# Head softmax on one core: GpSimd issues its adding DMA ahead of the weighing of an older unit

## The chip, the core and the metric

The kernel runs on one core of one Trainium2 chip. The metric is the device time of one execution in microseconds (us). Four compute engines matter here: TensorE (PE; its weight loads are PEld), VectorE (DVE), ScalarE (ACT) and GpSimd (POOL). SyncE (SP) only issues DMAs. Each engine runs its own list of instructions in order; engines wait for each other on semaphores.

## The reference, cut to what matters

Two transformer layers on x of 4 x 1024 x 128: banded attention, a mixture of 32 experts, a second attention, and the experts again. Only the second attention is touched. Its softmax runs over the **heads**, not over the keys:

```
q = (x @ Wq.T + bq).reshape(B, S, H, D)              # 16 heads of 8
scores = jnp.einsum('bqnd,bknd->bnqk', q, k) / jnp.sqrt(jnp.float32(D))
attn = jax.nn.softmax(scores, axis=1)                # axis 1: the heads
out = jnp.einsum('bnqk,bknd->bnqd', attn, v)
```

So for every pair of a query and a key, 16 exponentials are summed over the heads, and each is divided by that sum.

## The kernel before

The stage is `head_softmax_attention`. Its work is cut into **units**: 128 keys by 128 queries by 16 heads. A chunk is one tile of 128 queries; it has 8 units, one for each tile of keys (`kt` 0 to 7). There are 4 batches of 8 chunks, so 32 chunks and `ALL` = 256 units. Each engine walks over the units with its own lag:

- **TensorE**, `chunk_of`: in its unit u it subtracts the maximum from the first half of the scores (`take_maximum`, line 912), makes the scores of the second half (`scores_of`, line 890), sums the quarters of unit u-4 into the denominator (`denominator_of`, line 922), makes the first half of the scores of u+1, subtracts the second maximum, and multiplies the weights of unit u-5 with the values (`attend`, line 905). At some `kt` the function `ahead` adds projections of later chunks and, at `kt` 6, the output of the chunk before (lines 928, 929).
- **ScalarE**: the exponential of the first half of unit u (line 1069), the copy of heads 0 to 7 of unit u-1 from `ex` to `half` (`copy_heads`, line 1032), for unit u-4 the logarithm of the denominator and two exponentials that make reciprocals, one in PSUM for VectorE (`recp`, line 1041) and one in SBUF for GpSimd (`recip`, line 1043), then the exponential of the second half of unit u.
- **VectorE**: the maxima of both halves (`largest`, line 1115), then heads 0 to 9 of unit u-4 times the reciprocal (`weigh`, line 1122), then now and then a small operation of `ahead`.
- **GpSimd**: three things for each step, each of another unit. `add_halves` (line 847) issues a DMA that adds heads 8 to 15 of `ex` onto the copy in `half`, inside SBUF; it waits for `copy_heads`. `add_quarters` (line 853) waits for that DMA to land and adds the upper half of `half` onto the lower, which leaves four slabs for TensorE. `weigh_rest` (line 859) waits for `recip` and weighs heads 10 to 15.

So one unit passes through copy, DMA, quarters, denominator, reciprocal, weighing and product with the values. `ex` has 6 buffers, `half` has 4, `recip` has 2. The order on GpSimd is written out by hand. In step s, before the change:

```
weigh_rest(s - 4)      # behind recip of unit s-4
add_halves(s - 1)      # behind the copy of unit s-1; issues its DMA
add_quarters(s - 2)    # behind the landing of the DMA of unit s-2
```

Of the kernel before, what the change touches and what calls it, by code (L numbers as in the profile page):

```python
# [715 lines left out]
def head_softmax_attention(nc, c, x, mv, ht, q_dram, k_dram, k_first, zero_f16, zero_f32):  # L716
# [8 lines left out]
    LAG, RING, SUMS = 4, 6, 4  # L725
    ON_DVE = 10
    BY_DMA = 0
    ALL = B * NQ * BT
# [4 lines left out]
    with Mem(nc, "head") as m:  # L733
# [39 lines left out]
        def copies(unit):  # L773

            return 3 * unit + (4 if unit < ALL - 1 else 3)
# [64 lines left out]
        @block.gpsimd  # L840
        def _(pool):
            m.start(pool, "pool")

            def add_halves(unit):

                pool.wait_ge(ex_ready, ONE + copies(unit))
                pool.dma_start(half[:, unit % SUMS, :, :], ex[:, unit % RING, 8:16, :], accum_op=ALU.add).then_inc(summed[unit % 2], 16)  # L847

            def add_quarters(unit):

                pool.wait_ge(summed[unit % 2], (unit // 2 + 1) * 16)
                hf = half[:, unit % SUMS, :, :]
                pool.tensor_tensor(hf[:, 0:4, :], hf[:, 0:4, :], hf[:, 4:8, :], ALU.add).then_inc(quarter_ready, 1)  # L853

            def weigh_rest(unit):

                pool.wait_ge(copy_ready, ONE + unit + 1)
                e = ex[:, unit % RING, ON_DVE:NH, :]
                pool.tensor_tensor(e, e, recip[:, unit % 2, :][:, None, :].broadcast_to([P, NH - ON_DVE, P]),  # L859
                                   ALU.mult).then_inc(rest_ready, 1)  # L860

            for step in range(ALL + LAG):
                if step >= LAG:
                    weigh_rest(step - LAG)
                if 0 < step <= ALL:
                    add_halves(step - 1)
                if 1 < step <= ALL + 1:
                    add_quarters(step - 2)

        @block.tensor  # L870
        def _(pe):
# [813 lines left out]
def build(nc, drams, x_dram, out):  # L1685
    with ExitStack() as ctx:
        c = {n: ctx.enter_context(nc.sbuf_tensor(f"c_{n}", s, dt)) for n, (s, dt) in SHAPES.items()}
        x = ctx.enter_context(nc.sbuf_tensor("x_tokens", [P, NT, E], F32))
        for n in WEIGHTS:
            c[n] = ctx.enter_context(nc.sbuf_tensor(f"c_{n}", [P, WEIGHTS[n], 2, P], F16))  # L1690
        for att in ("a_", "b_"):
            c[att + "bias"] = ctx.enter_context(nc.sbuf_tensor(f"c_{att}bias", [P, 2], F32))
        c["a_out"] = ctx.enter_context(nc.sbuf_tensor("c_a_out", [P, E], F32))

        mv = ctx.enter_context(nc.sbuf_tensor("moments", [P, NT, 2], F32))
        w_dram = nc.dram_tensor("pair_weights", [NPAIR, 2, T], F32).ap()

        q_dram = nc.dram_tensor("a_queries", [P, SLOTS, QCOLS], F16).ap()
        k_dram = nc.dram_tensor("a_keys", [P, SLOTS, KCOLS], F16).ap()
        v_dram = nc.dram_tensor("a_values", [LEFT + T + VTAIL, E], F32).ap()  # L1700
        with Mem(nc, "att_a") as m:
            bt = BandTensors(m)
            banded_attention(nc, c, x, mv, bt, q_dram, k_dram, v_dram, x_dram, drams)
        feed_forward(nc, "ffn1", c, x, mv, w_dram, True)
        bq_dram = nc.dram_tensor("b_queries", [P, SLOTS, P], F16).ap()
        bk_dram = nc.dram_tensor("b_keys", [P, SLOTS, P], F16).ap()
        zero_f16, zero_f32 = drams["zero_f16"], drams["zero_f32"][0:BT * (NH + 1) * VSLOT]
        bk_first = nc.dram_tensor("b_keys_first", [S // BLK, P, SLOTS, BLK], F16).ap()
        with Mem(nc, "att_b") as m:
            ht = HeadTensors(m)  # L1710
            head_softmax_attention(nc, c, x, mv, ht, bq_dram, bk_dram, bk_first, zero_f16, zero_f32)
        feed_forward(nc, "ffn2", c, x, mv, w_dram, False, out)
# [72 lines left out]
```

## Time and profile before

| | us |
|---|---|
| median of 3 runs | 1948.12 |
| their range | 1943.28 to 1952.0 |
| the profiled execution's own time | 1951.87 |
| its span, first to last instruction | 1950.1 |
| granted TensorE clock, mean over the span | 0.968 of full speed |

The profile page gives busy time by engine over the whole span; the stage in question lies between about 545 and 1641 us of it. Times in rows are us from the start of the span unless marked ns. In a timeline a row is start, duration, engine, line, operation, what it writes and reads, and in brackets how long the engine had been idle and who ended that. A GpSimd record can overlap the one before it by up to 0.3 us, so starts are the better measure there.

### The profile page before, as it was taken

The numbers are of one execution on the slowest core, as the hardware profiler recorded it, in microseconds if no ns is written. First come the engines' busy times: TensorE is split into PE (matmuls) and PEld (weight loads), VectorE is DVE, ScalarE is ACT, GpSimd is POOL, SyncE is SP. The second block draws the span as 40 slices with busy tenths as digits, with TensorE's granted clock in tenths as the row PEclk, the third lists the DMA queues.
The fourth block names the chain that finished last, engine by engine and source line by source line (L and its number), as shares of the span: only waits on it lengthen the run. The fifth ranks groups of instructions, "written<-read, shape, count | busy, mean of one in ns | idle before, by whom it ended". The sixth has DMA issues, their size and how long they took to land. (4 is left out here: it accounts for less than half of the span.)

```text
span 1950.1 us, 52397 instructions
## 1 busy us (share of the span) xinstructions
PE 1835.9 (94%) x20664; PEld 1154.3 (59%) x20664; DVE 1653.7 (85%) x2601; ACT 1434.7 (74%) x2473; POOL 1443.5 (74%) x1180
## 2 busy tenths in 40 slices
PE   5999799999789999999999999999999997999998
PEld 3666644444346666666666666666666665544443
DVE  6777688887679999999999999999999995788776
ACT  4566456666568888888888888888888884566665
POOL 6245256565349999999999989989999997456565
PEclk8999699999879999999999999999999997899999
DMA  6644176765267777777777667777767772677673
GB/s 162 195 110 105 27 150 140 135 141 113 81 140 141 143 136 140 136 139 139 139 136 142 133 134 144 139 136 139 137 125 138 135 134 56 130 151 154 124 133 56
DMA packets 156741, 253.07 MB, mean 130 GB/s; under 512 B 54736, under 2 KB 86368, under 8 KB 155760
## 3 DMA queue, kind: packets, MB, share of 16 engines
q0 software_dynamic: 36864, 134.23, 36.7%
q1 hardware_dynamic: 114112, 112.89, 26.7%
q8 instruction: 164, 2.69, 0.6%
q10 hardware_dynamic: 5520, 2.60, 0.5%
q14 instruction: 81, 0.66, 0.1%
HBM read 96.95 MB, written 18.55 MB: 59 GB/s over the span
## 5 line engine op out<-in xcount | busy, mean ns | idle before, releaser
L1115 DVE TENSOR_REDUCE head_shift<-head_score 128x64 bf16<-128x1024 f32 x512 | 625.8, 1222 | 74.4 <-PE head_score L890 48.2
L1069 ACT ACTIVATE head_ex<-head_score 128x1024 f32<-128x1024 f32 x512 | 521.1, 1018 | 121.5 <-PE head_score L912 120.9
L859 POOL TENSOR_TENSOR head_ex<-head_ex,head_recip 128x768 f32<-128x768 f32 x256 | 491.0, 1918 | 7.3 <-ACT head_recip L1043 6.6
L1371 POOL TENSOR_TENSOR ffn_sw<-ffn_sg,ffn_wide 128x512 f32<-128x512 f32 x256 | 324.9, 1269 | 218.4 <-ACT ffn_sg L1482 203.7
L853 POOL TENSOR_TENSOR head_half<-head_half 128x512 f32<-128x512 f32 x256 | 359.4, 1404 | 70.1 <-DMA head_half<-head_ex 67.8
L1122 DVE TENSOR_TENSOR head_ex<-head_ex,head_recp 128x1280 f32<-128x1280 f32 x256 | 378.2, 1477 | 10.0 <-ACT head_recp L1041 10.0
L912 PE MATMUL head_score<-head_shift,c_identb 128*128 128x512 bf16 x1024 | 311.7, 386 | 17.0 <-DVE head_shift L1115 11.7
L890 PE MATMUL head_score<-att_b_HB,att_b_GR 96*128 96x256 f16 x2048 | 312.4, 275 | 1.4 <-ACT head_ex L1069 1.4
L922 PE MATMUL head_den<-head_half,c_ident 128*128 128x128 f32 x2048 | 281.6, 281 | 20.2 <-POOL head_half L853 19.3
L847 POOL DMA_DIRECT2D head_half<-head_ex x256 | 251.2, 981 | 47.3 <-ACT head_half L1032 47.3
L905 PE MATMUL head_outp<-head_ex,att_b_vs 128*32 128x128 f32 x8192 | 277.4, 277 | 0.0
L922 PEld LDWEIGHTS head_den<-head_half,c_ident 128*128 128x128 f32 x2048 | 251.6, 193 | 39.4 <-POOL head_half L853 36.1
L905 PEld LDWEIGHTS head_outp<-head_ex,att_b_vs 128*32 128x32 f32 x8192 | 210.2, 110 | 107.0 <-issue 106.7
L1032 ACT ACTIVATE head_half<-head_ex 128x1024 f32<-128x1024 f32 x256 | 268.6, 1049 | 0.0
L1616 DVE TENSOR_TENSOR ffn_hidden<-ffn_sw,ffn_up 128x512 f32<-128x512 f32 x256 | 178.2, 696 | 93.1 <-POOL ffn_sw L1371 86.6
L1482 ACT ACTIVATE ffn_sg<-ffn_gate 128x512 f32<-128x512 f32 x272 | 162.4, 597 | 115.8 <-PE ffn_gate L116 114.7
L890 PEld LDWEIGHTS head_score<-att_b_HB,att_b_GR 96*128 96x128 f16 x2048 | 189.0, 98 | 88.2 <-ACT head_ex L1069 40.1
L1487 ACT ACTIVATE ffn_h_parts<-ffn_hidden 128x512 f16<-128x512 f32 x272 | 162.5, 597 | 97.4 <-DVE ffn_hidden L1616 90.6
L1624 DVE TENSOR_TENSOR ffn_h_parts<-ffn_hidden,ffn_h_parts 128x512 f16<-128x512 f32 x272 | 186.0, 684 | 0.1
L912 PEld LDWEIGHTS head_score<-head_shift,c_identb 128*128 128x128 bf16 x1024 | 66.9, 98 | 107.7 <-DVE head_shift L1115 83.9
L114 PE MATMUL ffn_down<-ffn_h_parts,c_down_parts 128*128 128x512 f16 x272 | 103.2, 379 | 3.3 <-DVE ffn_h_parts L1624 3.3
L114 PE MATMUL ffn_up<-ffn_xnT,c_up_parts 128*128 128x512 f16 x272 | 104.0, 382 | 0.6 <-DVE ffn_hidden L1616 0.3
(265 smaller groups left out, 2538.7 us busy)
## 6 DMA issues: line engine op xcount, KB each, us to landing
head_half<-head_ex POOLq DMA_DIRECT2D x256, 512.0 KB, 5.0
ffn_wide<-pair_weights SPq DMA_DIRECT2D x256, 256.0 KB, 9.7
band_v_windows<-a_values SPq DMA_DIRECT2D x24, 192.0 KB, 4.8
att_b_vs<-in_zero_f SPq DMA_DIRECT2D x2, 2176.0 KB, 10.0
a_keys<-band_parts_k SPq DMA_DIRECT2D x12, 295.5 KB, 2.5
att_a_HB<-a_keys SPq DMA_DIRECT2D x48, 73.9 KB
a_queries<-band_parts_q SPq DMA_DIRECT2D x12, 271.5 KB, 2.9
att_a_GR<-a_queries SPq DMA_DIRECT2D x12, 271.5 KB
```

What stands on the lines that cost most here:

```text
L847: pool.dma_start(half[:, unit % SUMS, :, :], ex[:, unit % RING, 8:16, :], accum_op=ALU.add).then_inc(summed[unit % 2], 16)
L853: pool.tensor_tensor(hf[:, 0:4, :], hf[:, 0:4, :], hf[:, 4:8, :], ALU.add).then_inc(quarter_ready, 1)
L859: pool.tensor_tensor(e, e, recip[:, unit % 2, :][:, None, :].broadcast_to([P, NH - ON_DVE, P]), ALU.mult).then_inc(rest_ready, 1)
L890: last = pe.matmul(score[:, h, g // 2, (g % 2) * GH * QS:(g % 2 + 1) * GH * QS].rearrange("p (a w) -> p a w", a=GH), GR[:, buf, g, kt * P: ...
L905: last = pe.matmul(outp[g * 32:(g + 1) * 32, 0:P], vs[:, buf * BT + kt, at:at + 32], ex[:, unit % RING, i, :], start=(kt == 0 and n4 == 0) ...
L912: last = pe.matmul(score[:, h, k, :].rearrange("p (a w) -> p a w", a=NH // 2), c["identb"][:, :], shift[:, h, :][:, None, :].broadcast_to( ...
L922: last = pe.matmul(den[:, 0:P], c["ident"][:, :], half[:, unit % SUMS, k, :], start=(i == 0), stop=(i == len(SLABS) - 1))
L1032: act.activation(half[:, unit % SUMS, BY_DMA:8, :], ex[:, unit % RING, BY_DMA:8, :], ACT.Copy).then_inc(ex_ready, 1)
L1069: act.activation(ex[:, unit % RING, :, h * QS:(h + 1) * QS].rearrange("p (a g) w -> p g a w", g=NG), score[:, h, :, :].rearrange("p k (g a ...
L1115: dve.tensor_reduce(shift[:, h, :], score[:, h, :, :].rearrange("p k (a w) -> p w k a", a=NH // 2), AX.XY, ALU.max, negate=True).then_inc( ...
L1122: dve.tensor_tensor(e, e, recp[:, 0:P][:, None, :].broadcast_to([P, ON_DVE, P]), ALU.mult).then_inc(prob_ready, 1)
L1371: pool.tensor_tensor(sw[:, unit % 2, :], sg[:, unit % 2, :], wide[:, k % 2, i, :], ALU.mult).then_inc(sw_ready, 1)
```

## The change

On GpSimd the weighing moves from the front of the step to its middle. Nothing else is changed: no size, no buffer, no instruction more or fewer, no other engine. The last steps are written out, so that the quarters of the last unit come ahead of the last three weighings.

```diff
@@ -859,13 +859,16 @@
                 pool.tensor_tensor(e, e, recip[:, unit % 2, :][:, None, :].broadcast_to([P, NH - ON_DVE, P]),
                                    ALU.mult).then_inc(rest_ready, 1)
 
-            for step in range(ALL + LAG):
+            for step in range(ALL + 1):
+                if step > 0:
+                    add_halves(step - 1)
                 if step >= LAG:
                     weigh_rest(step - LAG)
-                if 0 < step <= ALL:
-                    add_halves(step - 1)
-                if 1 < step <= ALL + 1:
+                if step > 1:
                     add_quarters(step - 2)
+            add_quarters(ALL - 1)
+            for unit in range(ALL + 1 - LAG, ALL):
+                weigh_rest(unit)
```

## Rows read from the trace of the kernel before

**Rows 1.** The page: busy time by engine, and two groups of the stage.
```profile
span 1950.1 us, 52397 instructions
PE 1835.9 (94%) x20664; PEld 1154.3 (59%) x20664; DVE 1653.7 (85%) x2601; ACT 1434.7 (74%) x2473; POOL 1443.5 (74%) x1180
...
L859 POOL TENSOR_TENSOR head_ex<-head_ex,head_recip 128x768 f32<-128x768 f32 x256 | 491.0, 1918 | 7.3 <-ACT head_recip L1043 6.6
...
L853 POOL TENSOR_TENSOR head_half<-head_half 128x512 f32<-128x512 f32 x256 | 359.4, 1404 | 70.1 <-DMA head_half<-head_ex 67.8
```

**Rows 2.** Windows: us, busy us of each engine, granted clock, DMA share, GB/s.
```profile
600.00:700.00 100.00, 98.17 (x1293) 68.23 (x1291) 95.34 (x92) 88.77 (x155) 94.15 (x74) 1.00 0.73 140
...
1100.00:1200.00 100.00, 96.24 (x1272) 66.77 (x1264) 92.49 (x90) 86.62 (x150) 92.57 (x72) 1.00 0.72 139
```

**Rows 3.** The tile head_half: landing of the DMA, and who waited (us, times).
```profile
L853 POOL TENSOR_TENSOR head_half<-head_half x256: 1257/1377/1592, 559.8 to 1630.0; 128x512 f32<-128x512 f32 x128
...
  PEld head_den L922: 36.1, 66
  PE head_den L922: 19.3, 29
  ACT head_lnd L1038: 16.4, 18
...
DMA to landing us min/median/max: 4.5/5.0/6.9
```

**Rows 4.** Timeline, all engines, a late landing and what followed.
```profile
867.00 0.97 POOL L847 DMA_DIRECT2D head_half<-head_ex  x1
...
869.08 1.97 POOL L859 TENSOR_TENSOR head_ex<-head_ex,head_recip 128x768 f32<-128x768 f32 x1
...
870.84 1.05 POOL L847 DMA_DIRECT2D head_half<-head_ex  x1
...
873.54 1.26 POOL L853 TENSOR_TENSOR head_half<-head_half 128x512 f32<-128x512 f32 x1 [1.65 <-DMA head_half<-head_ex]
...
874.77 1.81 POOL L859 TENSOR_TENSOR head_ex<-head_ex,head_recip 128x768 f32<-128x768 f32 x1
...
874.86 1.16 PE L922 MATMUL head_den<-head_half,c_ident 128*128 128x128 f32 x8 [0.56 <-POOL head_half L853]
...
876.49 1.23 DVE L1115 TENSOR_REDUCE head_shift<-head_score 128x64 bf16<-128x1024 f32 x1 [0.89 <-PE head_score L890]
```

**Rows 5.** Timeline, VectorE: the weighing of four units (24, 232 and 240 units after the first).
```profile
601.84 1.48 DVE L1122 TENSOR_TENSOR head_ex<-head_ex,head_recp 128x1280 f32<-128x1280 f32 x1
...
700.97 1.48 DVE L1122 TENSOR_TENSOR head_ex<-head_ex,head_recp 128x1280 f32<-128x1280 f32 x1
...
1574.71 1.48 DVE L1122 TENSOR_TENSOR head_ex<-head_ex,head_recp 128x1280 f32<-128x1280 f32 x1
...
1606.92 1.48 DVE L1122 TENSOR_TENSOR head_ex<-head_ex,head_recp 128x1280 f32<-128x1280 f32 x1
```

**Rows 6.** Timeline, all engines, a stretch without a late denominator.
```profile
931.94 1.48 DVE L1122 TENSOR_TENSOR head_ex<-head_ex,head_recp 128x1280 f32<-128x1280 f32 x1
...
933.86 1.05 ACT L1032 ACTIVATE head_half<-head_ex 128x1024 f32<-128x1024 f32 x1
...
934.81 0.87 POOL L847 DMA_DIRECT2D head_half<-head_ex  x1
...
935.33 0.29 ACT L1043 ACTIVATE head_recip<-head_lnd 128x128 f32<-128x128 f32 x1
...
935.42 1.57 POOL L853 TENSOR_TENSOR head_half<-head_half 128x512 f32<-128x512 f32 x1
...
936.66 2.10 POOL L859 TENSOR_TENSOR head_ex<-head_ex,head_recip 128x768 f32<-128x768 f32 x1
...
937.46 1.06 PE L922 MATMUL head_den<-head_half,c_ident 128*128 128x128 f32 x8
...
938.15 1.05 ACT L1032 ACTIVATE head_half<-head_ex 128x1024 f32<-128x1024 f32 x1
...
938.42 1.18 POOL L847 DMA_DIRECT2D head_half<-head_ex  x1
...
939.51 1.08 PE L905 MATMUL head_outp<-head_ex,att_b_vs 128*32 128x128 f32 x32
```

**Rows 7.** Line 859, all 256: duration in ns, min, median, max.
```profile
L859 POOL TENSOR_TENSOR head_ex<-head_ex,head_recip x256: 1800/1828/2126, 568.9 to 1634.4; 128x768 f32<-128x768 f32 x128
```

**Rows 8.** Timeline, all engines, the end of the stage.
```profile
1615.57 2.08 POOL L859 TENSOR_TENSOR head_ex<-head_ex,head_recip 128x768 f32<-128x768 f32 x1
...
1617.31 1.05 ACT L1032 ACTIVATE head_half<-head_ex 128x1024 f32<-128x1024 f32 x1
...
1620.01 1.06 ACT L1032 ACTIVATE head_half<-head_ex 128x1024 f32<-128x1024 f32 x1
...
1625.19 1.13 POOL L847 DMA_DIRECT2D head_half<-head_ex  x1
...
1627.41 1.97 POOL L859 TENSOR_TENSOR head_ex<-head_ex,head_recip 128x768 f32<-128x768 f32 x1
...
1630.05 1.26 POOL L853 TENSOR_TENSOR head_half<-head_half 128x512 f32<-128x512 f32 x1 [0.67 <-DMA head_half<-head_ex]
...
1631.37 2.07 PE L922 MATMUL head_den<-head_half,c_ident 128*128 128x128 f32 x8 [1.62 <-POOL head_half L853]
...
1633.37 6.08 PE L905 MATMUL head_outp<-head_ex,att_b_vs 128*32 128x128 f32 x160
...
1634.43 1.83 POOL L859 TENSOR_TENSOR head_ex<-head_ex,head_recip 128x768 f32<-128x768 f32 x1 [1.35 <-ACT head_recip L1043]
```

## The prediction

> **What bounds the stage now.** I read the page first. Over the span PE is busiest, but GpSimd's quarters (line 853) carry 67.8 us of waiting for their own DMA, while its weighing waits 6.6 us [rows 1]. The windows of the stage show PE and VectorE both above 92% at full clock, GpSimd about as full, and no engine quite at 100 [rows 2]. Such a picture is a ring of engines that pass one unit round, so I asked which wait starts the others. The rows of the tile `head_half` show it: the DMA takes 4.5 to 6.9 us to land, 5.0 in the median, and PE's denominator waited for the quarters in 66 and 29 records, 55 us together [rows 3].
>
> The timeline shows one such case from end to end [rows 4]. The DMA issued at 867.00 belongs to the quarters at 873.54: 6.54 us apart, because landing was late, and GpSimd stood idle for 1.65 us with the next weighing queued behind. PE's denominator started at 874.86, right behind the quarters; PE's scores followed it, and VectorE then sat idle for 0.89 us. Without such a case VectorE goes round in 4.1 us and is nearly full.
>
> There is a closed loop in the old order. Within a step GpSimd issues DMA u only after a weighing, and the weighing only after quarters u-2, which wait for DMA u-2. So two units can't take less than landing 5.0, plus quarters to weighing 1.23 (873.54 to 874.77), plus weighing to issue 1.76 (869.08 to 870.84) [rows 3, 4]: 8.0 us, or 4.0 a unit. A landing of 5.5 already makes 4.25. This is as long as the period of the other engines, so each late landing tells.
>
> **What the stage would take without these waits.** VectorE's weighing marks the units. Three chunks in a row, 24 units from 601.84 to 700.97, show no loss at all: 99.13 us, 33.04 a chunk, 4.13 a unit. In the last batch, which projects no keys or values ahead, an undisturbed chunk took 32.21 (1574.71 to 1606.92) [rows 5]. From 601.84 to 1606.92 there are 30 chunks in 1005.08 us. Of these 23 lie before the last batch and 7 in it: 23 x 33.04 + 7 x 32.21 = 985.4. The excess is 19.7 us, and I put it down to late quarters.
>
> **The change, part by part.** No instruction is added or removed. In the new order DMA u comes directly behind quarters u-2, and the weighing behind the DMA.
>
> *The DMA is issued earlier.* Its copy has long been ready: the issue at 938.42 is for the copy that ended at 934.91, 3.5 us before [rows 6]. The new loop for two units is 5.0 + 1.23 = 6.2 us, or 3.1 a unit, far below 4.0 (and a 6.9 us landing makes 4.1). Between issue u and quarters u now lie a weighing, quarters, an issue and another weighing, over a full period. In the clean stretch, with issues some 0.1 us behind their copies, 4.1 us apart, the quarters come about 2.7 us behind the next issue, so 6.8 us behind their own: only the longest landing is late, by 0.1.
>
> *Does GpSimd have room?* Near the end it runs nearly free: three units from 1615.57 to 1627.41 take 11.84 us, 3.95 each [rows 8]. That is less than 4.13, and 0.08 less than the last batch's 4.03. GpSimd will therefore catch up with ScalarE and wait for the copy instead, at the head of a step. This idle time costs nothing as long as the round holds.
>
> *What is queued behind that new wait.* The weighing, then the quarters. Take the copy that ended at 934.91 [rows 6]. Issue 935.0; its record is 0.87 long, so the weighing runs from about 935.9 (its reciprocal is ready at 935.62, 0.71 behind the copy) to 937.7, quarters to 938.9. The product that takes this weighing starts at 939.51, so 1.8 us of room where the old order had 0.75 (936.66 + 2.10 = 938.76). The denominator that takes these quarters is one period behind the one at 937.46, at about 941.6: 2.7 us of room. The issue is next wanted at the following copy's end, 939.20, and GpSimd is free at 938.9. Nothing is late; the smallest reserve is this last 0.3 us.
>
> *Does the moved weighing get dearer beside other work?* The page says 1918 ns in the mean, and the 256 records run from 1800 to 2126 ns [rows 1, 7], but two of different length (1.97 and 2.10) both have the next start 1.76 behind [rows 4, 6]; the rest is overlap in the records. Phases against VectorE vary through the stage in the old run, so the new phase costs nothing: 0 us, with a bound of 0.3 us x 256 = 77 us if all were paid at the long record's length. I take 0.
>
> By the Trainium skill, "SBUF — State Buffer", the section on the shared port pair, a VectorE operation with two SBUF inputs locks out GpSimd; VectorE's weighing takes its reciprocal from PSUM, and the narrow spread of starts agrees that nothing is blocked.
>
> *The tail.* The last copy ends at 1621.07, its DMA is issued only at 1625.19, quarters at 1630.05, denominator 1631.37, products 1633.37 to 1639.45 [rows 8]. In the new order the last issue waits for quarters that follow one weighing: the copy before it ended at 1618.36, so issue 1618.5, weighing to 1621.1, quarters to 1622.35, last issue 1622.35. It lands 5.0 later, at 1627.35; quarters to 1628.6; the denominator starts 2.8 us earlier than before. Three weighings now stand behind the last quarters, 1628.6 + 3 x 1.77 = 1633.9; the denominator ends 2.0 behind its start, at 1630.6, and the products of five units take 6.08, so the last unit's begin at about 1635.5. Hidden; 2.8 us gained.
>
> **Sum.** 19.7 + 2.8 = 22.5 us. On the profiled execution's own 1951.87 that gives 1929.4. That execution lies 3.75 above the median of the runs shown; from the median the same sum gives 1925.6. Part of the spread of those runs should be luck in landings, which the change takes away, so I take a value between, 1928. The rest of the program isn't touched.
>
> **Rivals.**
>
> *The wait only moves, no change.* The 19.7 us might not be GpSimd's: VectorE and PE, over 92% busy, could hold the round by themselves and the idle time could be theirs. For it: PE has its own pauses behind the scores. Against: the three clean chunks ran with the same PE and VectorE work [rows 5]. If half of the excess stays, the time is 1948 - 10 = 1938; if nearly all, 1943 to 1948.
>
> *The transfer is hidden anyway.* Then quarters never wait, and the reorder is worth 0, 1948 us. The row says 67.8 us of waits and 5.0 us for the landing [rows 1, 3], against it. By the Trainium skill, "DMA: Bandwidth & Descriptors", the section on the anatomy of one DMA, a transfer takes about 2.0 us plus its bytes over 436 GB/s; for these 512 KB that would be 3.2 us, an estimate by the page, and no quarters would wait. This trace disagrees, with 4.5 as the least.
>
> *GpSimd becomes the bound, slower.* The issue now waits for ScalarE at the head of a step, and each such wait empties GpSimd's queue, so the overlaps of 0.3 us in the records are lost, as would be any time between a semaphore and a start. At 3.95 + 0.1 it still fits. From 4.13 on it decides; the old mean, 1005.08 / 240 = 4.19 [rows 5], is break-even. At 3.95 + 0.3 + 0.1 = 4.35 the stage takes 0.16 x 256 = 41 us more, 1989. Against: after a DMA wait the old run restarts with start-to-start 1.23 and 1.76, no more [rows 4]. Its point is near, so it isn't nothing.
>
> *More than the sum.* If other engines' hidden waits for late quarters went as well, the 4.13 could fall to the last batch's 4.03: another 0.1 x 184 = 18 us, 1910. Against: that batch has less work ahead.
>
> **How the numbers follow.** The forecast has 0.72, between 1920 and 1936. Half or none of the gain (the first two rivals together) has 0.17, GpSimd as the bound 0.07, more than the sum 0.04. The range 1918 to 1943 takes in the forecast and about half of the first rival, 0.82. A measurement of this kernel can tell about 0.5%, so 9.7 us, from no change. Faster by more: 0.72 + 0.04 + a little of the half case, 0.77; within: 0.16; slower: 0.07.
>
> **What the new profile would show.** Right: line 853 waits for its DMA almost never; line 847 now waits for the copy (line 1032), 0.1 to 0.3 us in most units; PE's and PEld's waits for `head_half` fall from 55 us to a few in the tail; chunks of 33.0 us throughout, 32.2 in the last batch; the stage shorter by some 22 us with landings still near 5.0. Wrong: the chunks stay at 33.5 with new pauses of PE behind line 859 or of VectorE behind line 1041, or GpSimd without idle time at over 4.13 a unit, or landings that grow because two DMAs overlap longer.

## The result, and the profile after

The changed kernel takes 1931.76 us in the median of 5 runs (1926.64 to 1932.25), against 1948.12 us of 5 runs before (1943.07 to 1952.0). The ratio is 0.9915, 95% interval 0.989 to 0.994: 0.6 to 1.1% faster. The forecast was 1928, range 1918 to 1943. The profiled execution took 1932.25 us against 1951.87.

Lines from 862 on have moved by 3: 1069 is now 1072, 1122 is 1125, 922 is 925, 905 is 908. First the page of the changed kernel:

```profile
span 1930.4 us, 52397 instructions
PE 1826.9 (95%) x20664; PEld 1150.4 (60%) x20664; DVE 1655.3 (86%) x2601; ACT 1425.5 (74%) x2473; POOL 1452.1 (75%) x1180
...
L859 POOL TENSOR_TENSOR head_ex<-head_ex,head_recip 128x768 f32<-128x768 f32 x256 | 551.4, 2154 | 0.2 <-ACT head_recip L1046 0.2
...
L853 POOL TENSOR_TENSOR head_half<-head_half 128x512 f32<-128x512 f32 x256 | 405.7, 1585 | 0.7 <-DMA head_half<-head_ex 0.7
...
L847 POOL DMA_DIRECT2D head_half<-head_ex x256 | 234.5, 916 | 93.2 <-ACT head_half L1035 85.6
```

The same group in the page of the kernel before:

```profile
L847 POOL DMA_DIRECT2D head_half<-head_ex x256 | 251.2, 981 | 47.3 <-ACT head_half L1032 47.3
```

The wait of the quarters for their DMA has gone from 67.8 us to 0.7 [rows 1], and the issue now waits for its copy, which is what the new head of the step should do. Before, its 47.3 us were 3 waits at the very start of the stage; now 49.9 us are such a start, and 35.1 us are 91 short waits between 600 and 1585 us. The landing itself is no faster than before [rows 3], and who waited for `head_half` shows that the wait did not simply move to TensorE. The tile `head_half` of the changed kernel:

```profile
  PEld head_den L925: 5.7, 3
  PE head_den L925: 4.6, 2
...
DMA to landing us min/median/max: 4.5/5.1/7.1
```

TensorE waited 55 us for the quarters before, in 95 records; now 10 us in 5, all at the end of the stage. The weighings of VectorE mark the units, at the same four places as in [rows 5] (timeline of the changed kernel):

```profile
603.32 1.48 DVE L1125 TENSOR_TENSOR head_ex<-head_ex,head_recp 128x1280 f32<-128x1280 f32 x1
...
702.46 1.48 DVE L1125 TENSOR_TENSOR head_ex<-head_ex,head_recp 128x1280 f32<-128x1280 f32 x1
...
1558.10 1.48 DVE L1125 TENSOR_TENSOR head_ex<-head_ex,head_recp 128x1280 f32<-128x1280 f32 x1
...
1590.33 1.48 DVE L1125 TENSOR_TENSOR head_ex<-head_ex,head_recp 128x1280 f32<-128x1280 f32 x1
```

The first two marks are 24 units and 99.14 us apart; before they were 99.13, since this was the clean stretch. Over the 30 chunks from the first mark to the last it is 987.01 us for 1005.08: 18.1 us less. Over the first three batches the mean chunk is 33.03 us, so the clean chunk of 33.04 now holds there throughout, and nothing has become quicker than it; in the last batch it is 32.5.

How GpSimd now walks (timeline of the changed kernel, GpSimd alone):

```profile
904.16 0.88 POOL L847 DMA_DIRECT2D head_half<-head_ex  x1 [0.33 <-ACT head_half L1035]
904.83 2.06 POOL L859 TENSOR_TENSOR head_ex<-head_ex,head_recip 128x768 f32<-128x768 f32 x1
906.62 1.49 POOL L853 TENSOR_TENSOR head_half<-head_half 128x512 f32<-128x512 f32 x1
908.09 0.88 POOL L847 DMA_DIRECT2D head_half<-head_ex  x1
908.70 2.12 POOL L859 TENSOR_TENSOR head_ex<-head_ex,head_recip 128x768 f32<-128x768 f32 x1
910.49 1.56 POOL L853 TENSOR_TENSOR head_half<-head_half 128x512 f32<-128x512 f32 x1
912.66 0.88 POOL L847 DMA_DIRECT2D head_half<-head_ex  x1 [0.61 <-ACT head_half L1035]
```

The DMA issued at 904.16 belongs to the quarters at 910.49, 6.3 us later, with a weighing, other quarters, an issue and one more weighing between. A landing of 5.1 us, the median, is over 1.2 us before the quarters begin. The idle time of 0.3 or 0.6 us stands ahead of the issue, where it costs nothing. The records of the weighing have grown from 1918 to 2154 ns and those of the quarters from 1404 to 1585, yet nothing is slower: starts are still 1.79 apart from weighing to quarters. A GpSimd record begins while the one before still runs, so the busy time of the weighing's line has grown by 60 us without any more work; GpSimd as a whole shows 1452.1 us for 1443.5.

The end of the stage (timeline of the changed kernel, all engines):

```profile
1605.66 1.19 POOL L847 DMA_DIRECT2D head_half<-head_ex  x1
...
1610.58 1.26 POOL L853 TENSOR_TENSOR head_half<-head_half 128x512 f32<-128x512 f32 x1 [0.68 <-DMA head_half<-head_ex]
1611.81 3.58 POOL L859 TENSOR_TENSOR head_ex<-head_ex,head_recip 128x768 f32<-128x768 f32 x2
...
1612.55 2.05 PE L925 MATMUL head_den<-head_half,c_ident 128*128 128x128 f32 x8 [0.52 <-ACT head_lnd L1041]
...
1614.53 5.34 PE L908 MATMUL head_outp<-head_ex,att_b_vs 128*32 128x128 f32 x160
...
1619.94 0.28 ACT L1051 ACTIVATE head_outT<-head_outp 128x128 f32<-128x128 f32 x1 [4.43 <-PE head_outp L908]
```

From the last mark to the copy of the output it is 1619.94 - 1590.33 = 29.6 us. Before, with the same copy at 1639.53, it was 32.6: 3.0 us less. Counted from that mark, the last quarters start 2.9 us earlier (20.25 us behind it for 23.13 [rows 8]), but the last denominator only 2.2 us (22.22 for 24.45), because it now waits for the logarithm of the one before. The rest is in the 160 products, which take 5.34 us for 6.08. In both kernels they begin at a granted clock of 0.50 (1.2 GHz), after a stretch in which TensorE idled between denominators (in the changed kernel it was busy 1.16 of the 4.5 us from 1605.0 to 1609.5, the last before the clock fell). In the changed kernel the clock came back sooner: 0.67 in the mean from 1614.5 to 1617.0 us and 1.00 after it, against 0.50 from 1633.4 to 1636.0 and 0.92 up to 1639.4 before.

### The profile page after: what moved, and what is told of

Read it like the earlier page. It is cut to its first block and busy times, and to the rows that moved or that the text cites. A ratio compares the mean times of both kernels' runs of the same rounds, so it can differ in the third digit from the quotient of the medians.

```text
span 1930.4 us, 52397 instructions
## 1 busy us (share of the span) xinstructions
PE 1826.9 (95%) x20664; PEld 1150.4 (60%) x20664; DVE 1655.3 (86%) x2601; ACT 1425.5 (74%) x2473; POOL 1452.1 (75%) x1180
## 5 line engine op out<-in xcount | busy, mean ns | idle before, releaser
L859 POOL TENSOR_TENSOR head_ex<-head_ex,head_recip 128x768 f32<-128x768 f32 x256 | 551.4, 2154 | 0.2 <-ACT head_recip L1046 0.2
L853 POOL TENSOR_TENSOR head_half<-head_half 128x512 f32<-128x512 f32 x256 | 405.7, 1585 | 0.7 <-DMA head_half<-head_ex 0.7
L1125 DVE TENSOR_TENSOR head_ex<-head_ex,head_recp 128x1280 f32<-128x1280 f32 x256 | 378.2, 1477 | 7.7 <-ACT head_recp L1044 7.7
L847 POOL DMA_DIRECT2D head_half<-head_ex x256 | 234.5, 916 | 93.2 <-ACT head_half L1035 85.6
L925 PE MATMUL head_den<-head_half,c_ident 128*128 128x128 f32 x2048 | 272.8, 277 | 5.1 <-POOL head_half L853 4.6
```

The source lines that it names most:

```text
L925: last = pe.matmul(den[:, 0:P], c["ident"][:, :], half[:, unit % SUMS, k, :], start=(i == 0), stop=(i == len(SLABS) - 1))
L1125: dve.tensor_tensor(e, e, recp[:, 0:P][:, None, :].broadcast_to([P, ON_DVE, P]), ALU.mult).then_inc(prob_ready, 1)
```

## The experiments

Each ratio is against runs of the kernel before on the same chip; chips differ between groups of experiments, so ratios compare better than medians. "Mean chunk" is the distance of VectorE's marks 8 and 248, 30 chunks, divided by 30; it was 33.50 us before and is 32.90 with the change. "Quarters wait for DMA" is the time that line 853 waited for a landing, in us over the whole execution. "Tail" is from mark 248 to the copy of the output. These three are each read from one profiled execution.

| run | us, median | ratio (95%) | mean chunk | quarters wait for DMA | tail |
|---|---|---|---|---|---|
| the change | 1931.76 | 0.9915 (0.989 to 0.994) | 32.90 | 0.7 | 29.6 |
| e1_body_only | 1931.05 | 0.9916 (0.9893 to 0.9938) | 32.90 | 0.9 | 31.2 |
| e2_old_half_dma | 1932.91 | 0.9917 (0.9903 to 0.9932) | 32.90 | 0.3 | 30.7 |
| e3_new_half_dma | 1931.33 | 0.9909 (0.9893 to 0.9925) | 32.90 | 0 | 30.1 |
| e4_issue_quarters_weigh | 1955.0 | 1.0039 (1.0022 to 1.0056) | 33.71 | 63.2 | 29.9 |
| e5_new_ahead_early | 1913.15 | 0.9834 (0.9811 to 0.9856) | 32.34 | 0.7 | 30.0 |
| e6_old_ahead_early | 1941.53 | 0.9979 (0.9963 to 0.9995) | 33.25 | 63.2 | 31.6 |
| e7_new_on_dve_9 | 1952.73 | 1.004 (1.0022 to 1.0058) | 33.53 | 0.4 | 32.7 |
| e8_new_on_dve_11 | 1949.22 | 1.0024 (1.001 to 1.0037) | 33.53 | 1.2 | 28.9 |
| e9_early_and_tail | 1912.94 | 0.9838 (0.9814 to 0.9862) | 32.33 | 1.0 | 29.9 |
| e10_early_tail_both | 1911.04 | 0.981 (0.9783 to 0.9837) | 32.34 | 0.3 | 27.1 |

Two theories were put against each other. **The landing theory**: in the old order two units cannot take less than landing + quarters + weighing, about 8.0 us, and late landings held up the round. **The rival**: what helps is that the DMA is issued first in the step, ahead of a weighing, whatever the landing.

**e1_body_only.** The new steps with the old end.

```diff
-            add_quarters(ALL - 1)
-            for unit in range(ALL + 1 - LAG, ALL):
+            weigh_rest(ALL + 1 - LAG)
+            add_quarters(ALL - 1)
+            for unit in range(ALL + 2 - LAG, ALL):
                 weigh_rest(unit)
```

> The new order in every step but the old order of the last ones: the weighing of unit 253 stands ahead of the quarters of unit 255 again. The landing theory (late landings held the round, and the tail is a small separate term) expects chunks of 33.04 us as with the full change, and an end of the stage within 1.5 us of the full change's, since the weighing fills the 0.7 us in which GpSimd waited for the last landing: 1930 to 1934 us. The rival that the new tail carries a good part of the gain expects 1938 or more.

The chunks are the change's, to 0.01 us. The tail is 31.2 us, 1.5 more than with the change and 1.5 less than before. That isn't the worth of the new end, though. The last denominator of e1 starts 22.60 us behind the mark, only 0.4 us later than with the change; the other 1.1 us are in its products (timeline of e1, TensorE):

```profile
1609.30 2.07 PE L926 MATMUL head_den<-head_half,c_ident 128*128 128x128 f32 x8 [0.89 <-POOL head_half L853]
1611.30 6.47 PE L909 MATMUL head_outp<-head_ex,att_b_vs 128*32 128x128 f32 x160
```

They take 6.47 us for 5.34, at a granted clock of 0.50 from 1611.3 to 1614.0 and 0.84 from there to 1617.8. So of the 2.2 us by which the change's last denominator is earlier, about 1.8 come from the new steps and 0.4 from the new end; the rest of the tail is TensorE's clock. In the time of the whole none of this can be seen. It is the body that makes the gain.

**e2_old_half_dma, e3_new_half_dma.** The transfer is halved, in the old and in the new order. Heads 12 to 15 are left out of the denominator, so these two kernels don't compute the reference's result; every other instruction stays.

```diff
-                pool.dma_start(half[:, unit % SUMS, :, :], ex[:, unit % RING, 8:16, :], accum_op=ALU.add)...
+                pool.dma_start(half[:, unit % SUMS, 0:4, :], ex[:, unit % RING, 8:12, :], accum_op=ALU.add)...
```

> The old order with the adding DMA cut to heads 8 to 11, 256 KB for 512 KB; heads 12 to 15 are left out of the denominator. The landing theory: with about 3.5 to 4 us of landing for 5.0 the loop over two units shrinks from 8.0 to below 7.0 us, so the old order too runs in chunks of 33.0 us, quarters hardly wait, and the time is 1929 to 1935 us. The rival (what helped is that the issue no longer stands behind the weighing, whatever the landing) expects no change, 1944 to 1950.

> The new order with the same half-size DMA (heads 12 to 15 left out of the denominator). The landing theory: landing has left the round, so nothing more is won in the chunks, 33.04 us each, and at most 1 or 2 us in the tail: 1928 to 1932. If the transfer still cost something in the new order, or DMA traffic slowed other engines, it would be below 1925.

The old order with the half-size DMA, the tile `head_half`, and its timeline on GpSimd:

```profile
  PE head_den L922: 5.6, 3
...
DMA to landing us min/median/max: 3.3/3.4/5.1
```

```profile
905.04 1.83 POOL L859 TENSOR_TENSOR head_ex<-head_ex,head_recip 128x768 f32<-128x768 f32 x1 [0.49 <-ACT head_recip L1043]
906.81 0.86 POOL L847 DMA_DIRECT2D head_half<-head_ex  x1
907.42 1.56 POOL L853 TENSOR_TENSOR head_half<-head_half 128x512 f32<-128x512 f32 x1
908.81 1.95 POOL L859 TENSOR_TENSOR head_ex<-head_ex,head_recip 128x768 f32<-128x768 f32 x1
```

With a landing of 3.4 us the old order runs in the same chunks as the new one. Its weighing waits for the reciprocal at the head of the step (0.49 us), the mark of an engine that is ahead, and its issue still stands behind the weighing. The new order gains nothing from the short transfer. So landing time is what the old order was held by, and what the new one takes off the round. The rival falls. Of the 1 or 2 us that e3 was allowed to gain in the tail nothing came: its last denominator starts 22.22 us behind the mark, as with the change, and its tail is 30.1 us for 29.6 because the products took 5.77 us.

**e4_issue_quarters_weigh.** Issue first as in the change, but the weighing last.

```diff
-                if step >= LAG:
-                    weigh_rest(step - LAG)
                 if step > 1:
                     add_quarters(step - 2)
+                if step >= LAG:
+                    weigh_rest(step - LAG)
```

> In each step issue, quarters, weighing: the issue comes first as in the new order, but the quarters that wait for the last landing follow at once and the weighing is behind them. The landing theory: the loop over two units is again landing 5.0 + quarters 1.23 + weighing 1.77 = 8.0 us, and the weighing ends later than in the old order, at the limit of what the product with the values wants: no faster than before, 1945 to 1975. The rival that it is enough to issue first expects 1928 to 1935.

It is 0.4% slower than before. Who waited for line 859, none in the kernel before, and the waits for the DMA (of this run, two views of lines and tiles):

```profile
who waited for it (us, times):
  PEld head_outp L908: 18.1, 30
  PE head_outp L908: 10.0, 16
```

```profile
its engine sat idle before it (us, times) until:
  DMA head_half<-head_ex: 63.2, 93
  ACT head_half L1035: 56.5, 23
```

Both halves of the expectation are there. The order around the ring (weighing, issue, quarters) is the old one, with the weighing a place later; the loop over two units is unchanged, and so is the wait for the DMA. The weighing is so late that the product with the values waits for it, 28 us in 46 records. What the change has right is not that the issue is first, but that a weighing lies between an issue and the quarters of the unit before.

**e5_new_ahead_early, e6_old_ahead_early.** On TensorE, `ahead` goes where TensorE waits for a maximum.

```diff
+                    ahead(b, q, kt)
                     take_maximum(unit, 1)
...
                         attend(unit - (LAG + 1), n - 1 if back else n, (kt - LAG - 1) % BT, 1 - buf if start and back else buf)
-                    ahead(b, q, kt)
```

> The new order, and on TensorE the projections and outputs of other chunks are put ahead of the second maximum, where TensorE waits for VectorE by 0.3 to 0.4 us in most units, rather than behind the product with the values. If the clean chunk of 33.04 us is set by TensorE and VectorE in turn, with TensorE's extra work on that path, four units of a chunk lose 0.15 us or so and the one with the output up to 0.4: chunks of 32.2 to 32.6, 1914 to 1925 us. If VectorE alone sets it (it has small extra operations in six of the eight units), little changes: 1927 to 1932. If GpSimd, 3.9 a unit, is the next bound, chunks stay at or above 31.6.

> The same move on TensorE with the old order on GpSimd. The landing theory: the loop of 8.0 us for two units, 32.0 a chunk plus late landings, does not move, so less is won than in the new order, 0 to 10 us, and waits for the DMA grow over the 67.8 us of the kernel before: 1938 to 1948. If landing did not hold the old order, this would win as much as the same move in the new order.

With the new order this is worth another 0.8%, and 1913.15 us lies 0.85 below the range that was expected. The waits between 600 and 1500 us; the changed kernel first:

```profile
PEld head_score L915 <- DVE head_shift L1118: 77.6, 238, 0.6
POOL head_half L847 <- ACT head_half L1035: 34.6, 90, 0.6
```

```profile
PEld head_score L915 <- DVE head_shift L1118: 51.2, 190, 0.6
...
POOL head_half L847 <- ACT head_half L1035: 8.2, 26, 0.3
```

The second fence is e5's. The wait of TensorE's weight loads for the maximum is used up by a third, the undisturbed chunk is 32.38 us (633.08 to 665.46 on VectorE) for 33.04, and GpSimd's spare time falls from 34.6 to 8.2 us, so GpSimd is now nearly a bound. With the old order (e6) the same move shortens the mean chunk by only 0.25 us, not 0.56, and wins 0.2%. TensorE's and the weight loads' waits for the quarters in e6 come to 22.9 and 47.6 us over the whole, 70 for 55: the gain runs into the landing. One detail of the expectation was wrong: GpSimd's own wait for the DMA did not grow, it was 63.2 us. The late quarters show at TensorE instead.

**e7_new_on_dve_9, e8_new_on_dve_11.** One head moved from VectorE to GpSimd, and the other way.

```diff
-    ON_DVE = 10
+    ON_DVE = 9
```

In e8 the new value is 11.

> The new order with one head moved from VectorE's weighing (9 heads) to GpSimd's (7 heads). GpSimd's step grows from about 3.9 by 1.77 / 6 = 0.3 to 4.2 us and passes 4.13, so GpSimd is the bound: 256 x 0.07 to 0.1 = 18 to 26 us slower than the change, 1948 to 1960, and no waits of line 847 for the copy. If GpSimd has more room than that reckoning says, 1925 to 1935.

> The new order with one head moved from GpSimd (5 heads) to VectorE (11 heads). VectorE's weighing grows by 1.477 / 10 = 0.14 us; if VectorE sets the clean chunk in every unit, 256 x 0.14 = 36 us slower, 1962 to 1970; if TensorE's order sets part of the units, less, 1940 to 1960. GpSimd's waits for the copy grow by about 0.4 us a unit.

GpSimd in e7 (timeline, GpSimd alone):

```profile
902.10 2.72 POOL L847 DMA_DIRECT2D head_half<-head_ex  x1
902.71 4.24 POOL L859 TENSOR_TENSOR head_ex<-head_ex,head_recip 128x896 f32<-128x896 f32 x1
904.77 3.41 POOL L853 TENSOR_TENSOR head_half<-head_half 128x512 f32<-128x512 f32 x1
906.45 2.57 POOL L847 DMA_DIRECT2D head_half<-head_ex  x1
```

GpSimd is the bound here: it never waits for a copy in the stage's body, records overlap by 2 us, and the mean chunk of 33.53 us is 4.19 a unit at each place, the last batch too. The ends of the records (start plus duration) show it best. By starts the two issues shown are 4.35 us apart, and over the stage such distances run from 3.86 to 5.39; their ends are 904.82 and 909.02, 4.20 apart, and over the stage always 4.17 to 4.22: 2.12 for the weighing, 1.23 for the quarters, 0.84 for the issue. The weighing of 7 heads should take 1.77 x 7 / 6 = 2.07 us, 0.30 more, so the step with 6 heads is 4.19 - 0.30 = 3.89 us by this run. That is the reserve the prediction had asked about: 3.89 against 4.13. The kernels with 6 heads agree: there the shortest distance from one issue's end to the next is 3.9 us, before the change as after it. By starts the kernel before would look as if a step could take 3.60.

In e8 VectorE has 0.13 us more a unit (1610 ns for 1477), 34 us in all, but only 17 us are lost against the change, so about half of the added work falls into time in which VectorE doesn't set the length. e5 shows that TensorE's extra work sets part of the units; that these are the same units isn't shown. The waits for the copy grew by 0.29 us a unit (160.5 us for 85.6), the length of one head, where about 0.4 had been expected.

**e9_early_and_tail, e10_early_tail_both.** e5 with the end of the stage changed: on TensorE each of the last denominators is followed by a product; e10 also has e1's order on GpSimd.

```diff
             for kt in range(BT - LAG, BT):
                 denominator_of(LAST * BT + kt)
-            for kt in range(BT - LAG - 1, BT):
-                attend(LAST * BT + kt, LAST, kt, (B - 1) % 2)
+                attend(LAST * BT + kt - 1, LAST, kt - 1, (B - 1) % 2)
+            attend(LAST * BT + BT - 1, LAST, BT - 1, (B - 1) % 2)
```

> The new order with TensorE's extra work ahead of the second maximum, and at the end of the stage each of the last four denominators is followed by the product of the unit before, where the change had TensorE idle for 2.7 and 1.8 us and then made five products in 5.3 us. The chunks should stay at 32.4 us. If the last denominators are what the end waits for, the products of three or four units move into the gaps: 3 to 4 us less from the last chunk to the output, and 1908 to 1911 us against the 1913 without it. If the last weighings on GpSimd are the end (two of them stand behind the last quarters when its reciprocal is ready), it gains less than 2 us.

> As the kernel before, and on GpSimd the weighing of unit 253 put back ahead of the last quarters. If what held the products of units 252 and 253 at the end was that their weighings stood behind the last landing, from the last chunk's mark to the copy of the output (29.9 us) 2 to 3 us go, 1907 to 1911 us. If the tail is set by the last quarters, denominator and weighing whatever stands between, it stays within 1 us of that.

In e9 the tail stays: 29.9 us. The products do go into the gaps but then wait there (timeline of e9, all engines):

```profile
1588.68 1.27 POOL L853 TENSOR_TENSOR head_half<-head_half 128x512 f32<-128x512 f32 x1 [1.01 <-DMA head_half<-head_ex]
...
1589.91 3.57 POOL L859 TENSOR_TENSOR head_ex<-head_ex,head_recip 128x768 f32<-128x768 f32 x2
1591.77 0.43 PEld L908 LDWEIGHTS head_outp<-head_ex,att_b_vs 128*32 128x32 f32 x12 [2.38 <-POOL head_ex L859]
```

The weighing of unit 253 stands behind the last quarters, which wait for the landing. That is the new end of the change, harmless as long as all products come last. With that weighing put back (e10) the tail is 27.1 us. e10 is the fastest kernel of the study: 1911.04 us, 0.981 (0.9783 to 0.9837) of the kernel before. Its difference to e5 of 2 us is seen in the tail and not beyond doubt in the times.

## Why the prediction was right

- **The loop over two units, landing 5.0 + 1.23 + 1.76 us.** Right, and shown from three sides: a shorter landing frees the old order (e2), it gives the new order nothing (e3), and an order with the same loop keeps the wait (e4).
- **The excess of 19.7 us.** 18.1 were found. The clean chunk of the first batches was right to 0.01 us. The other 1.6 us are the last batch: one clean chunk of 32.21 had been taken for all seven, and with the change they take 32.5; that one was the last before the end of the stage, where work ahead runs out.
- **The tail, 2.8 us.** 3.0 were found, and that they agree is partly luck. The last issue and the last quarters came 2.9 us earlier, as reckoned. The denominator should have followed with 2.8 and had 2.2, since the sum left out its wait for the logarithm of the one before; and the products, taken at 6.08 us again, took 5.34 because TensorE's clock came back sooner.
- **Sum 22.5 us.** On profiled executions 19.6 us: 18.1 + 3.0, less 1.5 us by which the first mark came later (571.19 for 569.71), before any of the changed work had mattered. The medians differ by 16.4. Each profiled execution was the slowest of its five; the sum had been worked out from the one before, and the value between the two bases, 1928, was 3.8 us low. So the sum holds for the execution that it was read from, and a typical one of the kernel before probably had less to lose.
- **Luck in landings as part of the spread.** Nothing speaks against it: 25 runs of the kernel before on one chip lie 13.9 us apart, and the other two kernels whose quarters wait for the DMA 13.7 (e6, 12 runs) and 11.2 (e4, 9 runs). Those without that wait lie 1.3 to 7.8 us apart, the half-size transfers closest (e3 1.3, e2 2.1), though in fewer runs. No trace of a second execution shows it directly.
- **Where the idle time goes.** Right in kind: GpSimd waits for the copy, at the head of a step. But it does so in 91 steps of some 240 with 0.4 us each, not in most with 0.1 to 0.3: in half of the steps it takes its shortest time of 3.9 us and only catches up. The size "0.1 us behind the copy" was off too: after a wait the issue starts 0.30 us behind it. Neither cost anything at this reserve.
- **The moved weighing costs nothing.** Right; the dearer records (2154 ns) are overlap. By the ends of the records the shortest step is 3.90 us in both orders.
- **GpSimd as the bound**, decided at 4.13 us a unit: it did not come about. The distance was nearly as reckoned, 3.9 us for the 3.95 taken from starts. One head more (e7) puts it over and takes all of the gain away.
- **More than the sum, chunks below 33.04**: no. It took another edit, of TensorE's order (e5).
- **The DMA's duration.** Measured were 5.0 us for 512 KB and 3.4 for 256 KB. The Trainium skill, "DMA: Bandwidth & Descriptors", the section on the anatomy of one DMA, has about 2.0 us plus bytes over 436 GB/s, by which this DMA would take 3.2 us, an estimate by the page. e2, whose median landing of 3.4 us is near that, shows what the kernel before would then have looked like: nothing left to gain.

## What to carry to other kernels

Where one engine both issues a transfer and works on its result, count what lies between an issue and the use of what it brings, and write the loop down: landing plus everything that stands between that use and the next issue, over the number of transfers in flight. If it comes near the period of the round, even a median landing that fits leaves the late ones to be paid for: here 67.8 us of waits cost 18 us in the round. A piece of ready work moved between issue and use bought its own length for nothing, and from then on other engines' orders were worth tuning: the same edit on TensorE won 0.2% ahead of this change and 0.8% behind it.

## What the runs showed of the hardware that was not expected

- Halving the adding DMA within SBUF from 512 to 256 KB took the median landing from 5.0 to 3.4 us. By these two, 1.6 us for 256 KB is 164 GB/s, with 1.8 us that don't depend on the size: an estimate, and not of a DMA alone. The issues are 4.1 us apart, so a landing of 5.0 overlaps the next one. From 600 to 700 us the 16 DMA engines were busy 0.73 of the time with the full size [rows 2] and 0.42 with the half size (e2, e3), so most of the DMA traffic of the stage is this transfer.
- When GpSimd is the bound, its records begin up to 2.2 us before the one ahead has ended (e7), and their ends are the measure: the issues' ends are 4.17 to 4.22 us apart where their starts are 3.86 to 5.39 apart. An issue's record of 2.72 us stands for 0.84 of work. The landing looks longer too, 6.4 us in the median for 5.0, since it is counted from the record's start, and the issues' records are 1.5 us longer in the mean (2443 ns for 916).
- An issue on GpSimd that had waited for ScalarE started 0.29 to 0.30 us behind the end of the copy (91 waits of the change); a weighing there started 0.07 to 0.09 behind its reciprocal (107 waits of e2).
